# A decoder layer's cross-attention on TensorE: the projections dealt otherwise over the slots, and the second maxima product of a beat set behind its projection part

## What is computed

```python
q = x_q @ w_q
k, v = jnp.split(x_kv @ w_kv, 2, axis=-1)
logits = jnp.einsum('bhqd,bhkd->bhqk', q, k) * SCALE + bias     # bias: linear in (row - key), per head
attn = jax.nn.softmax(logits, axis=-1)
out = jnp.einsum('bhqk,bhkd->bhqd', attn, v)                    # then heads side by side
return out @ w_proj
```

## Time and profile before

| what | value |
|---|---|
| median of 3 runs | 1381.65 us (1378.21 to 2889.5) |
| the profiled execution | 1378.97 us, span 1377.4 us |
| cross-attention on TensorE, first to last matmul | about 341 to 1136 us of the span |
| its batches 1 to 6 (24 slots) | 490.2 to 1046.7 us |
| TensorE busy over the span | 1198.6 us (87%) |
| granted TensorE clock, mean | 0.948 |

### The profile page before, as it was taken

One profiled execution on the slowest core, in us unless ns is written; L12 is line 12 of the kernel. 1 busy time (PEld: TensorE's weight loads), 2 busy tenths in 40 slices (PEclk: granted clock), 3 DMA queues, 4 the chain that ended last, 5 costly groups with the idle time before them and its releaser, 6 DMA issues. The chain is left out here.

```text
span 1377.4 us, 24731 instructions
## 1 busy us (share of the span) xinstructions
PE 1198.6 (87%) x9295; PEld 915.0 (66%) x9322; DVE 821.0 (60%) x1522; ACT 590.6 (43%) x955; POOL 515.8 (37%) x411
## 2 busy tenths in 40 slices
PE   4799989994689998999999989999999863599997
PEld 3687868882577777777777777777777643344443
DVE  5767646654356646465656465565654616688884
ACT  2222222231235444444444444454444324577775
POOL 0011111114006565656565646555655651001110
PEclk9899999997699999999999999999999855999999
DMA  5222242224413243344252532442423208212211
GB/s 159 87 74 86 77 139 96 82 90 137 124 47 102 51 131 94 77 118 101 63 144 55 126 102 68 118 105 60 120 74 87 61 0 327 84 54 69 69 61 38
DMA packets 72362, 129.42 MB, mean 94 GB/s; under 512 B 18572, under 2 KB 30988, under 8 KB 71739
## 3 DMA queue, kind: packets, MB, share of 16 engines
q1 hardware_dynamic: 60595, 106.43, 27.5%
q0 software_dynamic: 11680, 21.81, 5.0%
HBM read 68.96 MB, written 11.22 MB: 58 GB/s over the span
## 5 line engine op out<-in xcount | busy, mean ns | idle before, releaser
L1177 DVE TENSOR_REDUCE xa_m_part<-xa_psM 112x1 f32<-112x376 f32 x512 | 265.4, 544 | 258.9 <-PE xa_psM L1323 257.6
L1020 POOL TENSOR_TENSOR xa_p_sum<-xa_p_sum,space 125x896 f32<-125x896 f32 x128 | 270.1, 2110 | 124.0 <-ACT space L1101 118.6
L1101 ACT ACTIVATE space<-xa_psS 125x448 f32<-125x448 f32 x384 | 207.1, 544 | 237.0 <-PE xa_psS L1307 228.5
L1323 PE MATMUL xa_psM<-xa_k,xa_q 104*112 104x376 f32 x512 | 162.7, 356 | 21.8 <-DVE xa_m_part L1177 20.4
L1307 PE MATMUL xa_psS<-xa_q,xa_k 104*125 104x224 f32 x768 | 147.9, 278 | 0.0
L1307 PEld LDWEIGHTS xa_psS<-xa_q,xa_k 104*125 104x125 f32 x768 | 140.8, 194 | 8.2 <-issue 1.4
L1323 PEld LDWEIGHTS xa_psM<-xa_k,xa_q 104*112 104x112 f32 x512 | 89.6, 178 | 46.8 <-DVE xa_m_part L1177 32.8
L1345 PE MATMUL xa_psO<-space,cv 125*32 125x224 f32 x1536 | 97.9, 375 | 1.8 <-ACT space L1101 1.1
L1293 PE MATMUL xa_psR<-xa_cT_hi,w_hi 128*128 128x376 f32 x256 | 87.5, 342 | 9.7 <-DVE xa_cT_lo L1167 9.7
L1293 PE MATMUL xa_psR<-xa_cT_hi,w_lo 128*128 128x376 f32 x256 | 93.0, 363 | 0.0
L1293 PE MATMUL xa_psR<-xa_cT_lo,w_hi 128*128 128x376 f32 x256 | 86.5, 338 | 0.0
(11 more groups left out here) (200 smaller groups left out, 2646.8 us busy)
## 6 DMA issues: line engine op xcount, KB each, us to landing
xa_k<-xa_k_st SPq DMA_DIRECT2D x384, 94.0 KB, 2.2
xa_q<-xa_q_st SPq DMA_DIRECT2D x192, 56.0 KB, 2.0
cv<-in_ctx_dram POOLq DMA_DIRECT2D x7, 1500.0 KB, 23.2
cv<-in_L_ffn_w_gate_dram SPq DMA_DIRECT2D x8, 512.0 KB, 4.9
cv<-in_L_ffn_w_up_dram SPq DMA_DIRECT2D x8, 512.0 KB, 6.1
cv<-in_L_ffn_w_down_dram SPq DMA_DIRECT2D x8, 512.0 KB, 7.1
ff_w_raw<-in_L_ffn_w_gate_dram SPq DMA_DIRECT2D x4, 1024.0 KB, 9.2
ff_w_raw<-in_L_ffn_w_up_dram SPq DMA_DIRECT2D x4, 1024.0 KB, 14.0
```

Source lines behind the costliest of these rows:

```text
L1020: nc.gpsimd.tensor_tensor(p_sum[:], before, tile, ALU.add).then_inc(p_summed, 1)
L1101: nc.scalar.activation(pT[:, (s + i) % 2, j], psS[0:KB, (HG * i + j) % NB, 0:2 * N], ACT.Exp).then_inc(exp_done, 1)
L1177: V.tensor_reduce(m_part[:, seg, t, jj:jj + 1], psM[0:T, seg, 0:SEG], AX.X, ALU.max, negate=True).then_inc(mx_read, 1)
L1323: M.matmul(psM[0:T, seg, 0:SEG], q4[0:ROWS, g, jj, t * T:(t + 1) * T], k4[0:ROWS, g % 2, jj, seg * SEG:(seg + 1) * SEG], start=True, stop= ...
```

## The change

It does four things. (1) `fill`: Y0 and Y1 stand at beats 6 and 11 of slot 0, Xa and Xb at 9 and 10; q2 and q3 leave slot 0 for slot 2; in slot 1 the r and q jobs alternate at the start, V0 comes from slot 2 and r5 goes there; K0a and K0b begin at beats 3 and 6 of slot 2, not 0 and 3. (2) `halves_at`: beats 0 to 11 get 2, 1, 1, 1, 1, 2, 2, 1, 2, 1, 1, 1 halves (before: 1, 1, 2, 1, 2, 1, 2, 1, 2, 1, 2, 0). (3) Where a beat has two, TensorE makes the second behind the filler, and VectorE reduces it, and joins at beat 11, behind its take and divide. (4) GpSimd issues the context load for batch b+2 behind slot 3 of batch b, not behind the first `split_heads` of batch b+1; and V jobs wait for the r job that read their rows.

```diff
--- before.py
+++ after.py
@@ -803,8 +803,8 @@
     BEATS = 16
 
 
-    halves_at = [range(0, 1), range(1, 2), range(2, 4), range(4, 5), range(5, 7), range(7, 8), range(8, 10),
-                 range(10, 11), range(11, 13), range(13, 14), range(14, 16)] + [range(0)] * 5
+    counts = (2, 1, 1, 1, 1, 2, 2, 1, 2, 1, 1, 1)
+    halves_at = [range(sum(counts[:k]), sum(counts[:k + 1])) for k in range(BEATS)]
     unit_at = [(k // HG, k % HG) if k < UNITS else None for k in range(BEATS)]
     attend_at = {5: 0, 9: 1, 13: 2}
     DENOMINATORS_AT = 2
@@ -813,9 +813,9 @@
 
     parts_of = {"V": 3, "K": 3, "Y": 3, "q": 1, "r": 1, "X": 1}
     fill = [
-        {0: "K2a", 3: "K2b", 6: "Xa", 7: "Xb", 8: "Y0", 11: "q2", 12: "q3", 13: "Y1"},
-        {0: "K3a", 3: "K3b", 6: "r0", 7: "r1", 8: "q0", 9: "r2", 10: "r3", 11: "q1", 12: "r4", 13: "r5"},
-        {0: "K0a", 3: "K0b", 6: "V0", 9: "V1", 12: "V2"},
+        {0: "K2a", 3: "K2b", 6: "Y0", 9: "Xa", 10: "Xb", 11: "Y1"},
+        {0: "K3a", 3: "K3b", 6: "r0", 7: "q0", 8: "r1", 9: "q1", 10: "r2", 11: "r3", 12: "V0", 15: "r4"},
+        {0: "q2", 1: "r5", 2: "q3", 3: "K0a", 6: "K0b", 9: "V1", 12: "V2"},
         {0: "K1a", 3: "K1b", 6: "V3", 9: "V4", 12: "V5"},
     ]
     first_fill = ["r0", "r1", "r2", "r3", "r4", "r5", "K0a", "K0b", "Xa", "Xb", "q0", "q1", "K1a", "K1b", "q2", "q3"]
@@ -1037,8 +1037,6 @@
                 for s in range(NG):
                     if (b, s) != (0, 0):
                         split_heads(*((b, s - 1) if s > 0 else (b - 1, NG - 1)))
-                    if s == 0 and b >= 1 and b + 1 < B:
-                        load_context(b + 1)
                     if s == 1 and b >= 1:
                         store(b - 1)
                     if s == 3 and b + 2 < B:
@@ -1046,6 +1044,8 @@
                     sum_keys(b, s)
                     if b + 1 < B:
                         clear_shift(b, s)
+                    if s == NG - 1 and b + 2 < B:
+                        load_context(b + 2)
             split_heads(B - 1, NG - 1)
             store(B - 1)
             pool.wait_ge(stored, B * DMA)
@@ -1212,14 +1212,17 @@
                     n = NG * b + s + 1
                     for k in range(BEATS):
                         if n < NG * B:
-                            for half in halves_at[k]:
+                            for half in halves_at[k][:1]:
                                 reduce_half(n, half)
-                            if k == TURN_AT - 1:
-                                join_maxima(n)
                         if ended := ended_before(b, s, k):
                             take(*ended)
                         if k == DENOMINATORS_AT and (b, s) != (0, 0):
                             divide(*((b, s - 1) if s > 0 else (b - 1, NG - 1)))
+                        if n < NG * B:
+                            for half in halves_at[k][1:]:
+                                reduce_half(n, half)
+                            if k == TURN_AT - 1:
+                                join_maxima(n)
                         if b + 2 < B and s == 2 and k == TURN_AT:
                             statistics(b + 2)
                         if b + 2 < B and s == 3 and k == TURN_AT:
@@ -1275,6 +1278,8 @@
                     right = lambda i, k: (xT_hi, xT_lo)[i][:, k, :]
                 elif what[0] == "V":
                     t = int(what[1])
+                    if part == 0:
+                        pe.wait_ge(read[bank_of[f"r{t}", b]], use_of[f"r{t}", b])
                     out = out[0:KB, :]
                     left = lambda i, k: (cT_hi, cT_lo)[i][:, k, t * KB:(t + 1) * KB]
                     right = lambda i, k: (w_hi, w_lo)[i][:, 2, k, :]
@@ -1385,6 +1390,9 @@
                             denominators(*((b, s - 1) if s > 0 else (b - 1, NG - 1)))
                         if part := part_at(b, s, k):
                             do(*part)
+                        if n < NG * B:
+                            for half in halves_at[k][1:]:
+                                maxima_half(n, half)
             denominators(B - 1, NG - 1)
             for what in ("Y0", "Y1"):
                 for part in range(parts_of["Y"]):
```

## The result

The changed kernel takes 1385.55 us (median of 20 runs, 1380.09 to 2887.21), the one before 1379.02 (20 runs, 1374.41 to 2889.5): ratio 1.0053, 95% interval 1.0037 to 1.0068. It was forecast at 1360.4 and faster; it is half a per cent slower. One of the twenty runs on each side took over 2880 us; the ratio is of the others. The profiled execution took 1382.15 us, 3.2 more than the one before.

The account below looks back on a forecast made before the run. TensorE was taken to bound batches 1 to 6, only its waits being savable: 5.9 - 3.15 = 2.75 us a batch, 16.5 for six, plus 0.6 and 1.5, 18.6 off 1378.97: 1360.4 us, range 1346 to 1382.

Parts of the forecast that it names:

- What goes: TensorE's old waits in batches 1 to 6 of the cross-attention all end: 2.3 + 3.0 + 0.6 = 5.9 us a batch.
- five signs: No maxima wait at beat 4/5; none before K0a; batches about 90 us; slot 1: key DMA wait 1, turning 0.9.
- (b): Join behind a take: turning waits 0.9 us in slot 1, 0.25 in slot 0, 0.05 in others; Y1's bank 0.3.
- (a): Slot 1's first maxima product waits 1.2 us a batch for head 0's third key DMA; bounds 0 to 4.
- (c): Slot 1's beats with only four transposes bring half 10, q0 and r3 early: 0.4 us, bounds 0 to 1.4.
- The load: Earlier context load ends ScalarE's wait for K2's key DMAs before K3a's take: 0.6 us a batch.
- rival B: K2's key DMAs decide, as slot 0 is shorter: 3.1 us a batch more, 1379.0 us; chance 0.12.
- what comes: New waits in batches 1 to 6, from key DMA, join, Y1's bank and short beats: 3.15 us a batch.
- rival A: Fewer new waits: 1.2 us a batch come, net 4.7, 1349 us; sign: batches of 88 or less; chance 0.22.
- batch 0: No Y there, so slot 0 has bare beats that take most of the gain of slots 1 to 3: 0.6 us won.
- batch 7: Y0 and Y1 cover slot 0's double beats, but slots 7.1 and 7.2 lack filler: 1.5 us won.
- C: Waits only move, join and short beats at upper bounds: 4.6 us a batch come for 5.9, 1369 us; chance 0.16.

Follow-up runs that it names:

- e1: The changed kernel with the join as a reduction with one SBUF input instead of two, same place: 1353.86 us, 0.9849 of the kernel before.
- e4: The kernel before with only the context load issued earlier, behind slot 3: 1376.75 us, ratio 0.9987.
- e7: The changed kernel with the join ahead of beat 11's take and the context load back at its old place: 1368.87 us, 0.9933 of the kernel before.
- e2: The changed kernel with the join, still with two inputs, ahead of the take at beat 11: 1353.26 us, 0.9819 of the kernel before.

## Why the prediction was wrong

**What goes, 5.9 us a batch: right.** All of the earlier trace rows went, at every place named. Of the five signs that the prediction named for being right, two are there: no wait at beat 4 or 5, and none before K0a. The other three are not: the batches take 92.5 us and not 90, the wait for the third key DMA stands once (0.4 us), since the longer turning hides it, and the turning in slot 1 waits 2.45 us and not 0.9.

**(b), the join, was the step that failed.** It was worked out as "product 0.33, reduction 0.54, r2's take 0.67, join 0.16", and the turning's waits as 0.9 in slot 1 and 0.25 in slot 0, within 0.3 to 2.0 for all. The last term was 2.07 and 1.97 us instead of 0.16. TensorE's idle time at the turning came to 2.1 us a place, 24.9 us in twelve (the earlier trace rows have none), so 4.5 us a batch with 0.17 for each; e1, with the block gone, has 3.2 us in six places, all in slot 1, 0.5 each. The chain itself was thus sized fairly (0.5 of idle time and 0.17 for what that figure leaves out, against 0.9), and slot 0's 0.25 did not come at all. Y1's bank, put at 0.3, is the wait for `xT_lo`: 0.2 and 0.17. The duration 0.16 had been read where the join stands alone; the bounds were made by moving whole terms, and no rival asked what runs on GpSimd in the beat that the join was moved to.

The trace of before had the evidence. Outside the stretch of the earlier trace rows three joins stand between 1063 and 1103 us:

```profile
L1181 DVE TENSOR_TENSOR xa_m_neg<-xa_m_part x3: 166/168/895, 1063.5 to 1102.9; 112x8 f32<-112x8 f32 x3
```

```profile
1080.01 6.43 POOL L1020 TENSOR_TENSOR xa_p_sum<-xa_p_sum,space 125x896 f32<-125x896 f32 x3 [1.33 <-ACT space L1101]
...
1083.40 0.90 DVE L1181 TENSOR_TENSOR xa_m_neg<-xa_m_part 112x8 f32<-112x8 f32 x1
```

One of them takes 895 ns, and it lies beside a sum, the second of three that take 6.43 us together; both end at 1084.3. That row against the 0.36 us of room would have given the blocked joins of slot 1, one a batch; in slot 0 the room was 1.05 us, and there too a take and a later reduction came ahead of the join. In the changed kernel 14 joins take 1.96 to 2.08 us, those of slots 0 and 1 of batches 0 to 6, and one takes 0.76, in slot 7.1. At 1.9 us more for each of the 14 that is up to 27 us. The executions show 32: some of each is covered, above all by the key DMA that slot 1 would wait for next, and the falls of the clock come on top.

The Trainium skill states it: "SBUF — State Buffer", section "Who interferes with whom", says that a VectorE instruction with two SBUF inputs contends with a GpSimd instruction that reads SBUF, that whichever is issued first has the shared ports for the whole instruction while the other blocks, and that a reduction with one input does not contend on trn2. The traces agree where they can: 2.07 us with two inputs beside a sum that was issued first, 0.16 with one input at the same place, and the end with the sum's. No run here has the join issued first and still under way when the sum comes.

**(a), the third key DMA, 1.2 us a batch.** In e1, where no turning hides it, TensorE idles 4.0 us for it in four places, some 0.8 us a batch with the 0.17 of each. The landing in slot 5.0 is 8.4 us with the early load and 9.2 with the old one, the last DMA's 7.2 and 10.5; over the six batches the means are 8.0 and 8.5, and 6.8 and 10.5. So the head start helps the third little and the last much. The term was oversized by some 0.4 us, not wrong. That packets take turns, which the prediction cites from the Trainium skill, "DMA: Bandwidth & Descriptors", section "Queues, rings and completion order", fits this better than arrival order. Neither says why, as the last section shows, the first two DMAs of a head land in 3 us beside the same load: the prediction's sentence that a key DMA beside the load takes four times its time holds for each third one only.

**(c), short beats.** TensorE shows no wait of its own there in e1's list; 0.4 a batch was too much.

**The load, 0.6 us a batch**, was right in kind for the kernel before (e4: 1.6 us in all by the medians, 5.2 in the profiled batches 1 to 6, for 3.6 forecast) and far too small for the changed one: 16 us. It was priced as the end of an old wait; with the new fill it is what keeps rival B away. B's mechanism is real: it is e7, with ScalarE standing six times. The change as made had its cure in it.

**The rivals.** Without the block, what comes was less than 3.15 us a batch: e1's batches 1 to 6 take 532.0 us, 88.7 each, near rival A's 88. Its gain in that stretch, 24.5 us, stands against the 16.5 forecast; batch 0 lost 0.6 instead of winning it, batch 7 won 3.3 instead of 1.5. So the forecast gain was somewhat too small for the kernel that it described, which is e1. None of the rivals was the one that came; C had the sign of it (waits of 5 us a batch under other names: here 26.5 + 19 x 0.17 = 29.7 us, 5.0 a batch), not the mechanism.

## What to carry to other kernels

When an instruction is moved, look at what the other engines do in the beat that it moves to, and whether it shares a port with them: here a VectorE instruction with two SBUF inputs, issued into a GpSimd one that reads SBUF, took the rest of that one's time, at 8 elements a partition. Read shortest, median and longest of a line over the whole trace, not a mean over the best stretch; two outliers in 32 (895 ns, and 406 in slot 0.0) told the mechanism here. Where such an instruction is on the path, turning it into a reduction over one SBUF input mended it (e1), which is safer than a place ahead of the sum, since the room that an order leaves (0.12 us at the narrowest in e2, worked out from the starts and ends of its joins and sums) may be gone with the next change. One tensor input is no safeguard by itself: the `tensor_scalar` of the normalising is stretched too (see below). And an edit that is worth 1.6 us alone, by the medians, may be worth 16 beside another: price it again in the kernel in which it will stand.

## What was not expected of the hardware

The join stood for 2.07 us at 8 elements a partition, 12 times its time alone; the sum beside it was not lengthened (2122 ns in the mean in 490 to 1046 us with the blocked joins, 2125 in e1 without).

In slot 3 of batches 0 to 5 the change carried another VectorE instruction into a sum: the second of the two `tensor_scalar` that normalise x (112x512 f32; one tensor and two columns of scalars, all from SBUF). It is issued 0.19 us after the sum has begun and takes 2.34 to 2.35 us instead of 0.54, ending 0.3 us after the sum. Which of its reads or writes meets the sum was not tried, and no run takes this stretch away, so what it costs, if anything, is not known.

Beside the context load not every key DMA is slow, but each third: in slot 3.0 of the changed kernel the third, sixth, ninth and twelfth land in 6.3 to 8.4 us, the eight others in 2.7 to 3.0. Of these the rows of the third and fourth together (7.7 and 2.9), and of the twelfth:

```profile
L941 SPq DMA_DIRECT2D xa_k<-xa_k_st x2: 592/595/598, 692.6 to 693.3; - x2
DMA to landing us min/median/max: 2.9/5.3/7.7
...
L941 SPq DMA_DIRECT2D xa_k<-xa_k_st x1: 591/591/591, 698.3 to 698.3; - x1
DMA to landing us min/median/max: 6.3/6.3/6.3
```

The third of each head writes rows 64 to 95 of `k4` (the loop in `pack_keys`), the first and second rows 0 to 63. Whether it is those rows, or what else, was not tried.
